# A macaron block on one core: causal masking moved from TensorE to GpSimd, the low parts of P moved to VectorE, the batch loops written out

## What is computed

```
x = x + 0.5 * ffn(layernorm(x))
x = x + attention(layernorm(x))
x = x + 0.5 * ffn(layernorm(x))

attention: q, k, v = tanh(x @ W + b), 16 heads of 64
           alpha = q k^T / 8, causal mask (key <= query), softmax over the keys
           ctx = alpha v;  result tanh(ctx @ Wo + bo)
ffn:       8 experts, each token goes to its best one, at most 320 per expert;
           relu(x @ w1 + b1) @ w2 + b2, weighted by the gate
```

## Time and profile before

| | |
|---|---|
| median of 3 runs | 537.52 us (536.99 to 538.22) |
| the profiled execution, its own time | 535.04 us |
| its span in the trace | 533.3 us |
| PE busy | 416.5 us, 78% |
| PEld busy | 286.7 us, 54% |
| DVE busy | 304.0 us, 57% |
| ACT busy | 254.4 us, 48% |
| POOL busy | 254.7 us, 48% |
| mean granted clock of PE | 0.93 of full |

### The profile page before, as it was taken

How to read it: one execution, slowest core, us unless ns; L and a number is a source line. 1 busy time by engine, 2 the same in 40 slices (tenths; PEclk the granted TensorE clock), 3 DMA queues, 4 the chain that set the end, 5 groups by cost and what they waited for, 6 DMA issues and landing times.

```text
span 533.3 us, 12440 instructions
## 1 busy us (share of the span) xinstructions
PE 416.5 (78%) x4337; PEld 286.7 (54%) x4337; DVE 304.0 (57%) x926; ACT 254.4 (48%) x441; POOL 254.7 (48%) x277
## 2 busy tenths in 40 slices
PE   1702999409699999999799999799999794089970
PEld 1601777305366766566466566466566562067850
DVE  6881345638966766488666488656488733222213
ACT  1100434007478877576577576577576611034310
POOL 6471155713665565256355556355556450204551
PEclk9999999858899999999899999899999987589995
DMA  8811344172000000000000000000000000125415
GB/s 271 274 55 53 108 137 115 37 264 74 1 2 1 2 2 1 1 4 1 6 2 2 20 3 1 6 2 2 20 3 1 2 22 0 43 67 155 130 53 166
DMA packets 31524, 28.16 MB, mean 53 GB/s; under 512 B 2732, under 2 KB 27365, under 8 KB 31208
## 3 DMA queue, kind: packets, MB, share of 16 engines
q1 hardware_dynamic: 27184, 19.97, 12.5%
q0 software_dynamic: 2560, 4.74, 2.7%
q10 hardware_dynamic: 1720, 2.66, 1.5%
HBM read 16.84 MB, written 10.52 MB: 51 GB/s over the span
## 4 chain that ended last, share of the span: by engine, by line
PE 40%; issue 21%; POOL 19%; DVE 12%; DMA 4%; ACTq 1%; ACT 1%; POOLq 1%; SPq 0%; DVEq 0%
POOL Pl L358 9%; PE pj L590 8%; PE sc L580 8%; PE sc L697 6%; POOL disp L330 4%; POOL Vl L358 3%; PE pj L667 3%; PE tT L542 2%; PE cx L717 2%; DVE X L959 2%; POOL r L324 2%; PE sc L702 2%; PE cx L719 2%; PE cx L718 2%; DVE Ph L1057 1%
## 5 line engine op out<-in xcount | busy, mean ns | idle before, releaser
L358 POOL TENSOR_TENSOR Pl<-Pf,Ph 128x512 f16<-128x512 f32 (+1 forms) x64 | 61.2, 970 | 78.0 <-DVE Ph L1057 78.0
L697 PE MATMUL sc<-Tq,Tk 64*128 64x128 f32 (+3 forms) x512 | 97.0, 477 | 0.0
L358 POOL TENSOR_TENSOR Pl<-Wf,Ph 128x512 f16<-128x512 f32 (+1 forms) x64 | 58.9, 935 | 55.7 <-DVE Ph L1057 55.7
L341 POOL DMA_INDIRECT ytok<-Y,who x48 | 49.5, 1032 | 68.6 <-DVE Y L925 56.2
L1057 DVE CAST Ph<-Pf 128x512 f16<-128x512 f32 (+1 forms) x96 | 55.0, 603 | 43.0 <-ACT Pf L491 42.4
L431 ACT ACTIVATE hT<-sc,RT 128x320 f32<-128x320 f32 x64 | 33.7, 527 | 91.9 <-PE sc L580 91.4
L717 PE MATMUL cx<-Vh,Ph 128*128 128x65 f16 x640 | 65.6, 196 | 12.5 <-POOL Vl L358 6.1
L1057 DVE CAST Ph<-Wf 128x512 f16<-128x512 f32 (+1 forms) x96 | 52.6, 578 | 26.0 <-ACT Wf L491 25.1
L717 PEld LDWEIGHTS cx<-Vh,Ph 128*128 128x128 f16 x640 | 59.2, 98 | 14.2 <-POOL Vl L358 6.5
L718 PE MATMUL cx<-Vl,Ph 128*128 128x64 f16 x640 | 65.6, 194 | 0.0
L719 PE MATMUL cx<-Vh,Pl 128*128 128x65 f16 x640 | 65.4, 194 | 0.0
(11 more groups left out here) (179 smaller groups left out, 845.5 us busy)
## 6 DMA issues: line engine op xcount, KB each, us to landing
W<-in_L_ffn_w SPq DMA_DIRECT2D x32, 256.0 KB, 2.7
disp<-empty SPq DMA_DIRECT2D x2, 1290.0 KB, 7.4
XE<-disp SPq DMA_DIRECT2D x16, 129.0 KB
ytok<-empty SPq DMA_DIRECT2D x2, 1024.0 KB, 12.5
G<-ytok SPq DMA_DIRECT2D x8, 256.0 KB, 3.7
out<-X SPq DMA_DIRECT2D x4, 256.0 KB, 2.4
ytok<-Y,who POOLq DMA_INDIRECT x48, 2.3
XE<-disp SPq DMA_DIRECT2D x16, 32.2 KB
```

Of the source, the lines that this page charges most:

```text
L341: pool.indirect_dma_start(ytok[phase], bass.IndirectOffsetOnAxis(ap=who[u][0:m, j:j + 1], axis=0), Y[u][0:m, j, :], None).then_inc(y_sc[u] ...
L358: pool.tensor_tensor(dst, src, hi, ALU.subtract).then_inc(done, 1)
L697: mm(score_bank(h, c)[:, o:o + w], Tk[u][half(h), P * kt:P * kt + P], Tq[u][half(h), P * kt:GN], start=kt == kts[0], stop=False)
```

## The change

Four things are done at once:

1. `identb`, `maskn` and the matmuls of L702 are gone. `scores` now raises `s_ps` with the last real score matmul.
2. POOL has a new function `causal`: behind each exp it sets P to zero where the key is later than the query, with one `affine_select` for a chunk and head on the 128x128 blocks of the diagonal (two blocks side by side for c1). It raises `masked`. DVE's casts wait for `masked` where they waited for `exp_done`.
3. All low parts of P are computed on DVE, right behind the casts of their chunk (`split_p`). POOL keeps those of V. `context` waits for one semaphore, `p_lo`.
4. The loops over the batches on PE, ACT, DVE and POOL are Python loops, so their code is written out.

```diff
-            pool.memset(identb[:], 0.0).then_inc(S["pool_const"], 1)
-            pool.memset(maskn[:], 0.0).then_inc(S["pool_const"], 1)
...
-            def p_low(s, u):
-                for c, h in POOL_LOWS:
-                    a, n, _ = CHUNKS[c]
-                    pool.wait_ge(S["p_hi"], 6 * s + 2 * c + h + 1)
-                    low(Pl[u][h][:, a:a + n], Pf[u][h][:, a:a + n], Ph[u][h][:, a:a + n], S["p_lo_p"])
+            def causal(s, u):
+
+                for c, (a, n, kts) in enumerate(CHUNKS):
+                    w = n if len(kts) == 1 else GN - P
+                    for h in range(2):
+                        pool.wait_ge(S["exp_done"], done_by(s, h, c))
+                        blocks = Pf[u][h][:, a:a + w * len(kts)].rearrange("p (t n) -> p t n", n=w)[:, :, 0:P]
+                        pool.affine_select(out=blocks, in_=blocks, compare_op=ALU.is_ge, fill=0.0, base=0,
+                                           pattern=[[0, len(kts)], [1, P]], channel_multiplier=-1).then_inc(S["masked"], 1)
...
                 if score:
-                    p_low(i - 1, 1 - u)
+                    causal(i - 1, 1 - u)
                     v_low(i - 1, 1 - u)
...
-            with pool.Fori(2, NG) as b:
+            for b in range(2, NG):
...
-            with act.Fori(1, NG) as b:
+            for b in range(1, NG):
...
                     for h in range(2):
-                        mm(score_bank(h, c)[:, o:o + w], Tk[u][half(h), P * kt:P * kt + P], Tq[u][half(h), P * kt:GN],
-                           start=kt == kts[0], stop=False)
-                for h in range(2):
-                    for kt in kts:
-                        o = KOFF[kt] - a
-                        last = mm(score_bank(h, c)[:, o:o + P], identb[:], maskn[:], start=False, stop=kt == kts[-1])
-                    last.then_inc(S["s_ps"], 1)
+                        last = mm(score_bank(h, c)[:, o:o + w], Tk[u][half(h), P * kt:P * kt + P], Tq[u][half(h), P * kt:GN],
+                                  start=True, stop=True)
+                        if kt == kts[-1]:
+                            last.then_inc(S["s_ps"], 1)
...
-                pe.wait_ge(S["p_hi"], 6 * c + h + 5)
-                pe.wait_ge(*low_part(c, h, 2))
-                pe.wait_ge(*low_part(c, h, 1))
+                pe.wait_ge(S["p_lo"], done_by(c, h, 2))
...
-            with pe.Fori(1, NG) as b:
+            for b in range(1, NG):
...
-            def split_high(s, u, c):
+            def split_p(s, u, c):
                 a, n, _ = CHUNKS[c]
+                part = slice(a, a + n)
                 for h in range(2):
-                    dve.wait_ge(S["exp_done"], 6 * s + 2 * c + h + 1)
+                    dve.wait_ge(S["masked"], done_by(s, h, c))
                     if not (isinstance(s, int) and s < 2):
                         dve.wait_ge(S["ctx_ps"], 2 * (s - 2) + h + 1)
...
+                for h in range(2):
+                    dve.wait_ge(S["p_hi"], done_by(s, h, c))
+                    dve.tensor_tensor(Pl[u][h][:, part], Pf[u][h][:, part], Ph[u][h][:, part],
+                                      ALU.subtract).then_inc(S["p_lo"], 1)
...
-            with dve.Fori(1, NG) as b:
+            for b in range(1, NG):
```

More of the change, by code:

```diff
@@ L61 @@
 CHUNKS = [(0, 512, [0]), (512, 512, [1, 3]), (1024, 256, [2])]
-ORDER = [(c, h) for c in range(3) for h in range(2)]
-POOL_LOWS = [(0, 0), (0, 1), (2, 0), (2, 1)]
-V_LOWS = [(1, 0), (1, 1)]
 X_STATS, X_APPLY, X_TURN = {0: 2, 1: 3}, {0: 1, 1: 2, 2: 3}, {1: 1, 2: 2, 3: 3}
@@ L214, in macaron, with done_by @@
         block = ctx.enter_context(nc.Block())
-        def low_part(s, h, c):
-            done, lows = ("p_lo_p", POOL_LOWS) if (c, h) in POOL_LOWS else ("p_lo_v", V_LOWS)
-            return S[done], len(lows) * s + lows.index((c, h)) + 1
+        def done_by(s, h, c):
+            return 6 * s + 2 * c + h + 1
         def score_bank(h, c):
@@ L296, in _ @@
             pool.memset(identf[:], 0.0).then_inc(S["pool_const"], 1)
-            pool.memset(identb[:], 0.0).then_inc(S["pool_const"], 1)
             pool.memset(onesb[:], 1.0).then_inc(S["pool_const"], 1)
-            pool.memset(maskn[:], 0.0).then_inc(S["pool_const"], 1)
             pool.memset(lower[:], 1.0).then_inc(S["pool_const"], 1)
[L301 to L306, removed]
+            pool.wait_ge(S["pool_const"], 3)
+            pool.affine_select(out=identf[:], in_=identf[:], compare_op=ALU.not_equal, fill=1.0, base=0,
+                               pattern=[[-1, P]], channel_multiplier=1)
             pool.affine_select(out=lower[:], in_=lower[:], compare_op=ALU.is_ge, fill=0.0, base=0,
@@ L314, in _ @@
             pool.memset(empty[:], 0.0).then_inc(S["pool_const"], 1)
-            pool.wait_ge(S["pool_const"], 6)
+            pool.wait_ge(S["pool_const"], 4)
             pool.iota(empty[:, :, P:ROW].bitcast(U32), [[1, SLOTS // P], [1, 1]], base=NTOK,
@@ L1049, in _ @@
             x_stats(1)
-            def split_high(s, u, c):
+            def split_p(s, u, c):
                 a, n, _ = CHUNKS[c]
+                part = slice(a, a + n)
                 for h in range(2):
-                    dve.wait_ge(S["exp_done"], 6 * s + 2 * c + h + 1)
+                    dve.wait_ge(S["masked"], done_by(s, h, c))
                     if not (isinstance(s, int) and s < 2):
                         dve.wait_ge(S["ctx_ps"], 2 * (s - 2) + h + 1)
-                    dve.tensor_copy(Ph[u][h][:, a:a + n], Pf[u][h][:, a:a + n]).then_inc(S["p_hi"], 1)
-            def split_low(s, u):
-                for c, h in V_LOWS:
-                    a, n, _ = CHUNKS[c]
-                    dve.wait_ge(S["p_hi"], 6 * s + 2 * c + h + 1)
-                    dve.tensor_tensor(Pl[u][h][:, a:a + n], Pf[u][h][:, a:a + n], Ph[u][h][:, a:a + n],
-                                      ALU.subtract).then_inc(S["p_lo_v"], 1)
+                    dve.tensor_copy(Ph[u][h][:, part], Pf[u][h][:, part]).then_inc(S["p_hi"], 1)
+                for h in range(2):
+                    dve.wait_ge(S["p_hi"], done_by(s, h, c))
+                    dve.tensor_tensor(Pl[u][h][:, part], Pf[u][h][:, part], Ph[u][h][:, part],
+                                      ALU.subtract).then_inc(S["p_lo"], 1)
             def normalise(c, u, h):
@@ L1082, in step @@
                 if score:
-                    split_high(i - 1, 1 - u, 0)
+                    split_p(i - 1, 1 - u, 0)
                 if mix:
@@ L1086, in step @@
                 if score:
-                    split_high(i - 1, 1 - u, 1)
+                    split_p(i - 1, 1 - u, 1)
                 if late:
@@ L1090, in step @@
                 if score:
-                    split_low(i - 1, 1 - u)
-                    split_high(i - 1, 1 - u, 2)
+                    split_p(i - 1, 1 - u, 2)
             def add_out(b):
```

9 lines of the change are left out of this document (3 added, 6 removed).

## The result

The changed kernel took 544.88 us (median of 4 runs, 540.37 to 547.66), the kernel before on the same chip 537.25: ratio 1.016, 95% interval 1.011 to 1.021. It is slower, where 526.3 and faster was predicted, and outside the range. The profiled execution took 544.78 us, with a span of 543.0 and a mean granted clock of 0.916.

A forecast was written before the change was run, and what follows sets the result against it. PE bounds ordinary steps before the change, DVE with POOL after it. Terms -10.6 (first cast at 149.52 to that at 388.21), -0.2 (to last context), -0.4 (start) and 0 sum to -11.2 us: 537.52 becomes 526.3, range 519 to 538.

The forecast's parts named there:

- walk through an ordinary step: Ordinary attention step on DVE and POOL, DVE a little behind: own work and waits for POOL come to 7.57 us.
- Mask matmuls, 0.57 us a step on PE: PE in an ordinary step: without the mask matmuls PE alone could do it in 7.40 us instead of 7.97.
- The selects at 0.29 and 0.42 us: POOL in a step: four one-block selects at 0.29 and two two-block ones at 0.42, 2.0 us in all.
- The first loop of the forecast: DVE's chain in an ordinary step: 6.02 us own work plus 0.08, 0.47 and 1.0 of waits, 7.57 us.
- The second loop: Ordinary step, PE's head 1 context to next first cast 4.48, then to DVE's normalisation end 2.95: 7.43 us.
- The step of 7.7 us: Ordinary step after the change: 7.57 plus one hand-over of 0.13, bound by DVE with POOL.
- rival 3: Hand-overs keep the ordinary step at 7.97, only the batches' ends gain: 532.5 us, chance 0.19.
- Steps 4 to 7 at 38.1: End of a batch on DVE's chain: 4 x 7.7, less 0.8, plus 8.1 of extras, 38.1 us.
- The loops' stops of 3.50 and 3.30: PE's standing still at its loop's two jumps back, 3.50 and 3.30 us: gone with written-out loops.
- Steps 0 to 2 of batch 0 at nothing: First batch: DVE subtracts 1.86 us more a step, POOL no longer holds it; change 0, 1.9 either way.
- V's low part at 1.0: POOL's low part of V comes between DVE's two casts of c2 and holds DVE for about 1.0 us.
- Rival 2: POOL's low part of V runs late, the next c0's select waits: steps of 8.55, 545.9 us, chance 0.14.

The follow-up runs named there:

- the normalisation first: Changed kernel with DVE's normalisation of head 0 put ahead of the two subtractions of c0 instead of behind them: 529.37 us, ratio 0.990.
- the narrow selects: Changed kernel with selects covering 2 columns of each block instead of 128, most of the mask missing from the output: 524.23 us, ratio 0.978.
- the loops alone: Kernel before with only its batch loops written out on all four engines: 525.77 us, ratio 0.982.
- the loops kept: Changed kernel with the batch loops of PE, ACT and DVE back, POOL's still written out: 546.07 us, ratio 1.022.

## Why the prediction was wrong

The step of the prediction that failed is its walk through an ordinary step: it puts the selects of c1 under the normalisation, where they would cost next to nothing, and they run beside the subtractions of c0. Term by term:

- **Mask matmuls, 0.57 us a step on PE: nearly right.** PE is busy 12 us less, and without masks and selects the step fell to 7.25 to 7.35, 0.6 to 0.7 less than 7.97.
- **The selects at 0.29 and 0.42 us, 2.0 a step: too cheap**, 0.41 and 0.60 in the mean. Where nothing ran beside them it was 0.29 and, for two blocks, 0.50 (0.99 for a pair, with the normalisation first), so most of this is waiting beside DVE's work, and only 0.08 for each of the two-block ones is a price of their own.
- **The place of c1's selects: wrong, and the step that failed.** The walk let POOL do the selects of c1 "under the normalisation", with 0.08 us left. But their exponentials are done when DVE begins with the subtractions of c0, and the normalisation stands behind those. So they ran beside the subtractions and stretched them by 0.42 us, inside the loop from context to context. The first loop of the forecast, 7.57, is DVE's own: measured against it, c1's selects took 0.42 for 0.08, those of c2 0.10 for 0.47 (the casts of c1, 0.77 for 0.66), V's low part 1.05 for 1.0, and DVE waited 0.18 for the second select of c0. The second loop was laid out rightly. Its first part, 2.95 us from first cast to the end of the normalisation, measured 3.27 (169.44 to 172.71): casts and wait 0.95 for 1.14, subtractions 1.62 for 1.20, normalisation 0.70 for 0.61. Its other part measured 4.54 for 4.48, and the hand-over to PE 0.15. Together 7.96 us, where 7.43 stood, and 7.7 was taken. The step that I had in mind is that of the version with the normalisation first: 7.78. That version has ratio 0.990 and the changed kernel 1.016; the 2.6% between them are 14 us, of the 18.6 by which the forecast was off.
- **The step of 7.7 us** was therefore 7.96, rival 3's 7.97. It equals the step before by coincidence: PE's work of 7.4 and half a microsecond of waits (0.16 and 0.35). The rival's reason, three hand-overs at 0.1, is not what was measured.
- **Steps 4 to 7 at 38.1: 41.2 and 40.8**, and behind the last batch 41.0 for 37.6. Four steps at 7.97 are 1.1 more. Up to 1.6 us is the granted clock, by what a fall of it cost with the narrow selects; the forecast had no term for it. Without selects 35.9 were measured, so the sum of extras alone was not too small.
- **The loops' stops of 3.50 and 3.30: gone as forecast.** I priced them inside DVE's chain, and the chain was longer than I had it.
- **Steps 0 to 2 of batch 0 at nothing, 1.9 either way: +5.1 us**, from the first combination of the experts' results (at 111.43 before, 110.42 after) to step 3: 38.1 and 43.2. How much of it is the change's stays open. Two of the experiments run the same code up to there, the loops alone that of the kernel before and the loops kept that of the changed kernel, and they took 39.9 and 41.6: the same code differs by 1.6 to 1.8 us. So the change's part is between 1.6 and 5.1 us, by which two of these are compared. PE waited 6.74 us at 146.09 for a normalisation of DVE; it also waited 6.01 there without selects, which took 40.9, so the selects make only a part of it. And the granted clock was 0.50 from 141.2 to 151.4 us, around that stop, where the kernel before had a mean of 0.84 from 141 to 152. The normalisation first took 39.5, 2.1 to 3.7 less. The bound of 1.9 was the subtractions of one step, without the selects, without what the order makes of them and without the clock.
- **V's low part at 1.0: the price was right**, 0.9 beside c2's casts. The place was not always: in the step shown it stands beside the subtractions of c1 (1.05). **Rival 2 did not come**: selects of c0 didn't wait for it; POOL had stood still for 1.92 us ahead of the one at 169.11. The slower side had another mechanism, and none of my rivals had it: selects beside subtractions ahead of a normalisation, dear at the batches' ends.

On the shared port the Trainium skill ("SBUF — State Buffer", Who interferes with whom) says that one operation locks the other out, as the casts of c2 beside V's low part show (1.41 us for 0.48). For select and subtraction the sum fits: 0.42 us more for a pair of subtractions is near the 0.50 of one select of two blocks alone. I had used the rule, but with the operations in the wrong place.

## What to carry to other kernels

When work moves to an engine that shares a port with the next one in the chain, lay both programs side by side in time and find what each operation runs beside; put operations that read PSUM there, and those with two SBUF operands elsewhere. The same change was 1.6% slower or 1% faster by the place of one normalisation. Test the parts of a change one by one: here the whole of the gain came from one of them, the loops.

## What the runs showed that was not expected

- A select's time in a group's mean hardly depended on its width, 0.29 to 0.33 us for 128 x 2 columns and 0.38 to 0.41 for 128 x 128, since the narrow ones waited beside subtractions. Alone they took 0.19 and 0.29, so 64 times the columns cost 0.10. A wide one slows a subtraction beside it; the narrow ones did not.
- The granted clock made 1.6 us of difference between equal stretches of one kernel (36.3 and 37.9 us with the narrow selects). With PE's stops in step 5 at 1.7 and 2.1 to 2.2 us (the changed kernel) it fell in all three stretches, with 1.4 and 1.7 us (no selects) in none, with 1.5 and 1.7 to 1.8 us (narrow selects) in two of three.
- Written-out loops brought 9 us where the two stops of PE were 6.8. Steps 4 to 7 of the two batches lost 5.6 and 6.3 us, of which some came back behind them. In the kernel before the granted clock was at half after each stop, for longer after the second; ScalarE's and VectorE's programs jump as well. What each of these is worth was not tested apart.
